# A state-space stage: ScalarE copies Y earlier in the slot, a block's last scan goes ahead of the next block's first product, and semaphores are cleared by ranges

## The reference

```python
def _selective_scan(x, dt, Bm, Cm, A, D):
    dA = jnp.exp(dt[..., None] * A)
    dBx = (dt * x)[..., None] * Bm[:, :, None, :]
    def step(h, inputs):
        dA_t, dBx_t, C_t = inputs
        h = dA_t * h + dBx_t
        y = jnp.einsum('bdn,bn->bd', h, C_t)
        return (h, y)
    ...
    return jnp.swapaxes(ys, 0, 1) + x * D[None, None, :]
...
y = _selective_scan(x, dt, Bm, Cm, A, D)
y = y * jax.nn.silu(z)
return y @ out_proj_w.T
```

## Time and profile before

| | us |
|---|---|
| median of 3 runs | 3063.39 (3062.54 to 3074.31) |
| the profiled execution, its own time | 3050.3 |
| its span, first to last instruction | 3048.6 |
| Mamba stage in it | 318.6 to 1367.6 |
| of which its 16 blocks of scans | 371.7 to 1361 |
| TensorE busy | 2538.4 (83%) |
| VectorE busy | 2301.2 (75%) |
| ScalarE busy | 1779.8 (58%) |
| GpSimd busy | 1383.6 (45%) |

### The profile page before, as it was taken

One profiled execution on the slowest core, in us unless ns is written; L12 is line 12 of the kernel. 1 busy time (PEld: TensorE's weight loads), 2 busy tenths in 40 slices (PEclk: granted clock), 3 DMA queues, 4 the chain that ended last, 5 costly groups with the idle time before them and its releaser, 6 DMA issues. The chain is left out here.

```text
span 3048.6 us, 38598 instructions
## 1 busy us (share of the span) xinstructions
PE 2538.4 (83%) x11128; PEld 1660.4 (54%) x11128; DVE 2301.2 (75%) x4133; ACT 1779.8 (58%) x3099; POOL 1383.6 (45%) x1486
## 2 busy tenths in 40 slices
PE   6888387878888889777887689969989889887999
PEld 5766143333344344226766568845655556554887
DVE  6788478999999999988787544477778777774444
ACT  3567465556557656524566445547767667765555
POOL 2365588988888888862464630021111111210000
PEclk9999688999999999997999789979999999997999
DMA  2246222222222222211245200020000000001000
GB/s 68 53 134 123 80 71 67 74 68 71 70 69 75 73 70 76 73 52 61 53 139 108 73 21 1 0 95 1 1 1 1 2 1 1 1 1 39 7 8 14
DMA packets 99805, 152.39 MB, mean 50 GB/s; under 512 B 12940, under 2 KB 50572, under 8 KB 99028
## 3 DMA queue, kind: packets, MB, share of 16 engines
q1 hardware_dynamic: 82052, 98.41, 10.5%
q0 software_dynamic: 17040, 51.07, 7.0%
q10 hardware_dynamic: 512, 0.53, 0.1%
HBM read 131.08 MB, written 18.87 MB: 49 GB/s over the span
## 5 line engine op out<-in xcount | busy, mean ns | idle before, releaser
L1730 POOL TENSOR_TENSOR a_hc<-a_H,a_cb 128x512 f32<-128x512 f32 x512 | 623.8, 1230 | 149.6 <-DVE a_H L1598 141.0
L1390 PE MATMUL a_Y<-a_hc,ident 128*128 128x512 f32 x1024 | 532.4, 633 | 51.3 <-POOL a_hc L1730 47.7
L2196 DVE TENSOR_REDUCE a_mx<-a_W 128x1 f32<-128x512 f32 (+3 forms) x768 | 397.1, 551 | 152.9 <-PE a_W L1985 99.0
L2096 ACT ACTIVATE a_pt<-a_W 128x512 f32<-128x512 f32 (+3 forms) x768 | 353.3, 493 | 221.1 <-PE a_W L1998 218.0
L1516 ACT ACTIVATE a_dA<-a_dt,a_aneg 128x512 f32<-128x512 f32 x512 | 340.4, 715 | 209.3 <-DVE a_H L1598 106.0
L1390 PEld LDWEIGHTS a_Y<-a_hc,ident 128*128 128x128 f32 x1024 | 187.0, 196 | 293.5 <-POOL a_hc L1730 185.0
L1998 PE MATMUL a_W<-a_Q,a_K 128*128 128x512 f32 (+3 forms) x768 | 301.5, 398 | 4.8 <-issue 2.7
L1982 PE MATMUL a_W<-a_K,a_Q 128*128 128x512 f32 (+3 forms) x768 | 272.5, 361 | 21.7 <-DVE a_mx L2196 10.9
L2337 POOL TENSOR_TENSOR a_spare<-a_zero 128x1 f32<-128x1 f32 x128 | 27.8, 217 | 575.5 <-ACT a_pt L2096 575.5
L1324 PE MATMUL a_Bp<-a_bcs,a_sel 128*128 128x512 f32 x256 | 179.4, 702 | 95.6 <-DVE a_H L1598 88.3
L712 POOL DMA_INDIRECT m_xg<-m_xrows,m_gidx x184 | 194.9, 1059 | 120.9 <-DVE m_didx L596 65.4
(11 more groups left out here) (330 smaller groups left out, 6332.7 us busy)
## 6 DMA issues: line engine op xcount, KB each, us to landing
a_cb<-a_crow SPq DMA_DIRECT2D x256, 256.0 KB, 3.1
m_orows<-m_yt SPq DMA_DIRECT2D x46, 256.0 KB
a_Q<-attention_zeros POOLq DMA_DIRECT2D x3, 2048.0 KB, 13.7
t_wst<-ternary_w SPq DMA_DIRECT2D x22, 256.0 KB, 2.7
m_xrows<-m_pool SPq DMA_DIRECT2D x16, 256.0 KB, 2.3
m_xg<-m_xrows,m_gidx POOLq DMA_INDIRECT x184
out<-x SPq DMA_DIRECT2D x8, 256.0 KB, 2.3
m_wg<-moe_ws SPq DMA_DIRECT2D x2, 516.0 KB, 4.5
```

What stands on the lines that cost most here:

```text
L1390: pe.matmul(Y[:, h, :], ident[:], hc[:, g % HCRING, :], start=False, stop=v == NS - 1).then_inc(s_y, 1)
L1730: pool.tensor_tensor(hc[:, G % HCRING, :], H[:, s, span], cb[:, v % RING, :], ALU.mult).then_inc(s_hc, 1)
L2096: act.activation(pt[:, u % PR, 0:BLK - r * P], W[:, 3 + u % 3, 0:BLK - r * P], ACT.Exp).then_inc(s_exp, 1)
L2196: dve.tensor_reduce(dst, W[:, s % 3, 0:min(BLK, (t + 1) * P - c * BLK)], AX, ALU.max)\
```

## The change

Three edits. ScalarE's copy of Y moves from behind the slot's reads of O and its decays to the head of the same slot. VectorE's last scan of a block, which stood behind the first product of the next block except in block 1, now precedes it in every block, and also its wait for `u`. And `Phase.clear` makes runs of adjoining semaphore numbers and clears each run with one instruction.

```diff
     def clear(self):
+        nums = sorted(s.num for s in self.sems)
+        first = [n for n in nums if n - 1 not in nums]
+        last = [n for n in nums if n + 1 not in nums]
         with self.nc.Block() as block:
             @block.gpsimd
             def _(pool):
-                for s in self.sems:
-                    pool.sem_clear(s)
+                for a, b in zip(first, last):
+                    pool.sem_clear(range(a, b + 1))
...
                     for v in range(NS):
+                        if v == 1 and b > 0 and (b - 1) % 4 in (0, 1):
+                            drain_y(b - 1)
                         for c in range(2):
...
                             decay(b, v + LEAD)
-                        if v == 1 and b > 0 and (b - 1) % 4 in (0, 1):
-                            drain_y(b - 1)
                         if slot_of(b, 2, "dt")(v):
...
                                 dve.wait_ge(s_B, b * NS + v + 1)
-                                if G == UB:
+                                if G and G % UB == 0:
                                     scan(G - 1)
                                 if G % UB == 0:
                                     dve.wait_ge(s_u, 2 * (b + 1))
                                 dve.tensor_tensor(product(G), u[:, b % 2, h, :], Bp[:, G // 2 % BRING, :],
                                                   ALU.mult).then_inc(s_bx, 1)
-                                if G not in (0, UB):
+                                if G % UB:
                                     scan(G - 1)
```

## The result

The changed kernel took 3035.6 us (median of 4 runs, 3027.2 to 3043.1) against 3063.0 before: ratio 0.9891, 95% interval 0.9868 to 0.9914, so 33 us faster by the ratio (26 to 40 by its interval, 27 by the two medians). The forecast was 33.0 us faster; that the two figures agree to the microsecond is luck, since the measurement is no finer than its interval. In a later set of runs the same kernel had 0.9886 (0.9869 to 0.9904).

A forecast was written before the change was run, and what follows sets the result against it. VectorE, 95% busy, was taken to bound the scan stage, and GpSimd's clears the seams. Clears 12.6, copy 17.5 and last scan 2.9 sum to 33.0 us off the 3063.4 median: 3030.4 us, range 3018 to 3046.

The forecast's parts named there:

- The clears: Seams between stages: range clears replace GpSimd's single semaphore clears, all on the path; 12.6 us, between 0 and 14.
- the lower end: Seams: a range clear of 48 semaphores costs as much as a single one now, 0.07 us.
- The end: Last seam: the final wait for the stores takes the clears' place, so only 0.3 of 1.7 us comes off.
- The copy: Scan stage, blocks 2, 6, 10, 14: copying Y earlier lets TensorE open the next Y sooner; 17.5 us.
- the four waits: VectorE's waits for Bp at the fifth slot of blocks 2, 6, 10 and 14; all go, 18.0 us.
- the chain: From the dt read through opening Y to the fifth slot's Bp and product: 5.8 us at full clock.
- Rival (b): Scan stage: the wait goes to another engine, GpSimd being late; the copy gives nothing, 3047.9 us; chance 0.11.
- rival (a): Scan stage: TensorE's clock stays low while Y is opened; 13.4 instead of 17.5 us, 3034.5 us; chance 0.13.
- The last scan: Block starts: the previous block's last scan fills VectorE's wait for `u`; 2.9 us, between 0 and 5.
- Rival (c): Seams: a range clear pays for each semaphore in it, so the clears gain nothing; 3043.0 us; chance 0.06.
- Rival (d): Scan stage: ScalarE, held at the copy, becomes late with the decays; slower, 3079.9 us; chance 0.03.

The follow-up runs named there:

- e7_copy_mid: Changed kernel with ScalarE's copy of Y behind the slot's reads of O and ahead of its decays; ratio 0.9894 to the kernel before.
- e3_scan: Kernel before with only VectorE's last scan of a block moved ahead of the next block's first product; ratio 0.9999.
- e2_copy: Kernel before with only ScalarE's copy of Y moved to the head of its slot; ratio 0.9956.

## Why the prediction was right

The sum and its parts came out near the forecast, 12.1 + 21.7 = 33.8 us by the profiles against 33.0. Part of that is luck: the copy gave less than its term, the last scan more.

- **The clears**, 12.6 us forecast, 12.1 by the profile. The mechanism held: nothing else runs in a seam. Two sizes were off and cancelled in part. A clear of 47 or 48 semaphores takes 0.29 us, not the 0.07 of the lower end; and there were eight ranges where I had allowed two a stage. The end gave 0.43, not 0.3.
- **The copy**, 17.5 forecast, 15.6 alone. Every one of the four waits went, and by the chain as it was counted: in the changed kernel the opening begins 0.05 us behind the dt read and the product could start 5.75 us behind it (1006.34 to 1011.25 + 0.84), counted 5.8. What failed is the step from waits to time: I took 18.0 less half a microsecond, as if TensorE's clock could change only in the four openings. It was low elsewhere instead: 2 us came back in blocks 4 and 6 through slower matmuls into Y, and 1.1 in blocks 0 and 1. Rival (b), that GpSimd would be late, did not occur.
- **The clock**, rival (a): full in the openings of blocks 2, 6, 10 and 14, in the changed kernel and in `e7_copy_mid`, as forecast. The rival saw only these four places; in the changed kernel the clock is low at blocks 3, 7 and 15 (0.50, 0.54 and 0.58). That idle time costs the clock was right on average only. The Trainium skill's rule ("TensorE: Matmul & The Clock Gate", Part 1: The HAM clock gate), that an idle TensorE falls to half rate, agrees with block 10 of the kernel before (0.66 behind 3.31 us of idle); block 2 of `e3_scan` had 1.00 behind as long an idle time, and all four openings of `e7_copy_mid` 1.00 behind 2.10.
- **The last scan**, 2.9 forecast, 5.1 alone by the profile, some 3.9 of it without the clock's part. The waits at 4, 8 and 12 shrank by 1.2 to 1.3, as counted. The part lost again was put too high: at block 8 it was the 0.4 us that I counted, but at block 12 nothing was lost in the changed kernel's first profile and 0.5 in the second. Block 3 had no wait for `u` in that trace; its 1.25 us ended with Bp. With both moves 21.7 us against 20.4.
- **Rival (c)** was half true: a range clear does pay for each semaphore, but 5.4 ns and not 65. **Rival (d)** did not occur, though its margin was thinner than I wrote: block 6 began at 770.8, not 772.6, so its Y ended 8.7 us into the block, not 6.9, with 10 as the limit. It did not come to that: with the copy first, the dt reads and the decays of blocks 2 and 10 stand where they stood relative to Y's end.
- **The base.** The sum was taken off the median of the timed runs. Against the profiled execution, 3050.3, the first profile of the changed kernel would have refuted it by 26 us, and wrongly: stages that were not touched vary by 6 to 15 us each.

## What to carry to other kernels

Where an engine idles although its input is ready, look whose program order holds the reader back: a copy out of an accumulator belongs right behind the work that completes it, ahead of anything that waits for the next round. Count the chain from the moved step to the bound engine with rows of the same chain elsewhere in the kernel, and then look which wait is next, since some of the gain can return there. Read the clock at the new wait before you name the engine behind it: here the waits that came back ended with inputs of GpSimd in the order, but GpSimd was on time and TensorE slow. And judge a gain of 1% by the window of the stage that was touched, or by many timed runs, and not by two profiled spans.

## What was not expected of the hardware

- One range clear of one semaphore took 37 ns, of 47 or 48 it took 288 to 289 ns: 5.4 ns for each further one ((289 - 37) / 47), far below the 65 ns from one single clear to the next.
- The same matmuls of the unchanged MoE stages had a granted clock of 0.90 and 0.87 in one set of runs and 0.97 and 0.92 in others, and took 6 and 12 us longer.
- Behind the same idle time for the copy, TensorE had full clock in block 2 of `e3_scan` and 0.55 in block 10. VectorE's wait there was 2.6 us shorter in block 2 and 1.4 us longer in block 10 than in the kernel before.
- Taking one idle stretch away did not take the low clock away. It turned up at other matmuls of the stage: 0.52 in block 4 of `e2_copy`, where the kernel before had 1.00, and 0.50 ahead of block 3's gate in the first profile of the changed kernel, where the second had 1.00.
